# A 16-sample, two-layer transformer kernel on one core: reciprocal deviations into PSUM, and a new written-out order of calls on every engine

## The reference

```python
h = _layernorm(x) * (1 + ca) + sa
x = x + ga * _L0_attn_ref(h, ...)      # 16 heads of 16, q/k normed, causal softmax
h = _layernorm(x) * (1 + cb) + sb
x = x + gb * _L0_ffn_ref(h, ...)       # 256 -> 1024 -> 1024 -> 1024 -> 256
...                                    # layer 1, with its own modulation:
x = x + ga * _L1_attn_ref(h, ...)      # h = A_bar*h + B_bar*x over t, 512 channels, 16 states
x = x + gb * _L1_ffn_ref(h, ...)       # rows and weights rounded to a 6-bit grid in blocks of 32
```

## Time and profile before

| what | value |
|---|---|
| median of three runs | 4414.48 us (4412.8 to 4420.98) |
| the profiled execution | 4410.43 us, its span 4408.7 us |
| TensorE busy | 3700.5 us, 84% of the span |
| VectorE busy | 3558.4 us, 81% |
| GpSimd busy | 2530.8 us, 57% |
| ScalarE busy | 2435.4 us, 55% |

### The profile page before, as it was taken

The page is one execution under the profiler, slowest core; times in us unless marked ns, Lnnn a source line. Parts: engine busy times, 40 slices in busy tenths (PEclk is TensorE's granted clock), DMA queues, the critical chain, the costliest instruction groups (busy, mean ns, idle before and its releaser), DMA issues. The chain is left out here.

```text
span 4408.7 us, 51342 instructions
## 1 busy us (share of the span) xinstructions
PE 3700.5 (84%) x17261; PEld 2188.9 (50%) x17261; DVE 3558.4 (81%) x3917; ACT 2435.4 (55%) x3413; POOL 2530.8 (57%) x1895
## 2 busy tenths in 40 slices
PE   5688888989899898989888898989989898998623
PEld 3364544636464554636464463646455463646301
DVE  4514788979898887989888897989889898988795
ACT  2344555647565565646555564656556564655532
POOL 0131756648484755758474674848475574847462
PEclk8697999999999999999999999999999999999856
DMA  4630211203030110203020120303011020302000
GB/s 176 228 106 1 78 34 39 77 6 111 1 101 15 63 53 25 92 6 111 1 90 27 38 78 6 111 1 101 15 63 53 26 90 6 111 1 87 15 5 5
DMA packets 69436, 247.79 MB, mean 56 GB/s; under 512 B 9600, under 2 KB 10112, under 8 KB 68736
## 3 DMA queue, kind: packets, MB, share of 16 engines
q1 hardware_dynamic: 66816, 235.28, 16.1%
q10 hardware_dynamic: 2304, 8.39, 0.5%
HBM read 212.19 MB, written 31.46 MB: 55 GB/s over the span
## 5 line engine op out<-in xcount | busy, mean ns | idle before, releaser
L668 POOL TENSOR_TENSOR kept<-kept,hb 128x512 f32<-128x512 f32 x640 | 809.5, 1300 | 28.2 <-DVE hb L1821 28.2
L1812 DVE TENSOR_TENSOR_SCAN hb<-ps,hb 128x512 f32<-128x512 f32 x640 | 741.8, 1203 | 6.5 <-ACT ps L1332 5.6
L636 POOL TENSOR_TENSOR kept<-kept,hb 128x1024 f32<-128x1024 f32 x128 | 334.8, 2632 | 698.1 <-DVE hb L1756 639.1
L881 PE MATMUL ps<-hid_bhi,wring 128*128 128x512 f32 x1536 | 623.2, 406 | 17.3 <-issue 13.8
L881 PE MATMUL ps<-hid_blo,wring 128*128 128x512 f32 x1536 | 608.0, 396 | 0.0
L1332 ACT ACTIVATE ps<-kept,a_neg 128x512 f32<-128x512 f32 x640 | 431.7, 691 | 263.3 <-DVE hb L1812 263.3
L621 POOL TENSOR_SCALAR_AFFINE_SELECT room<-room 128x512 f32<-128x512 f32 x256 | 237.8, 945 | 570.8 <-ACT room L1498 570.8
L1882 DVE TENSOR_REDUCE room<-ps 128x4 f32<-128x2048 f32 (+3 forms) x256 | 375.6, 1488 | 234.1 <-PE ps L1060 232.8
L881 PE MATMUL ps<-hid_ahi,wring 128*128 128x512 f32 x1280 | 514.4, 402 | 18.7 <-POOL hid_alo L683 17.9
L881 PE MATMUL ps<-hid_alo,wring 128*128 128x512 f32 x1280 | 503.5, 393 | 0.0
L1498 ACT ACTIVATE room<-ps 128x2048 f32<-128x2048 f32 (+1 forms) x192 | 305.3, 1590 | 256.7 <-PE ps L1086 256.1
(11 more groups left out here) (188 smaller groups left out, 7580.5 us busy)
## 6 DMA issues: line engine op xcount, KB each, us to landing
wring<-w_hi SPq DMA_DIRECT2D x352, 512.0 KB, 3.3
kept<-in_wffn SPq DMA_DIRECT2D x22, 512.0 KB, 6.0
w_hi<-wring SPq DMA_DIRECT2D x22, 512.0 KB, 6.9
w_lo<-wrest SPq DMA_DIRECT2D x22, 512.0 KB, 3.9
xn<-in_x_fm SPq DMA_DIRECT2D x17, 512.0 KB, 3.5
out_fm<-xc ACTq DMA_DIRECT2D x16, 512.0 KB, 5.1
room<-in_wmod SPq DMA_DIRECT2D x2, 1536.0 KB, 8.2
win<-in_win SPq DMA_DIRECT2D x1, 1024.0 KB, 8.4
```

The lines of the kernel that those rows point to most:

```text
L636: pool.tensor_tensor(pair_of(acc, h), pair_of(acc, h), pair_of(hb, h), ALU.add).then_inc(tail_acc, 2)
L668: pool.tensor_tensor(acc[:, m, :], acc[:, m, :], hb[:, s % 8, :], ALU.add).then_inc(acc_done, 1)
L881: mm = pe.matmul(bank(bk), wring[:, r % 3, at + k * P:at + (k + 1) * P], src[i][:, k, :], start=(k == 0 and i == 0), stop=(k == K - 1 and ...
L1812: dve.tensor_tensor_scan(hb[:, s % 8, :], bank(2 + m % 2), hb[:, s % 8, :], 0.0, ALU.mult, ALU.add).then_inc(scanned, 1)
```

## The change

Two parts. First, `Exp` of each layer norm writes the reciprocal deviation over the variance in its PSUM bank, and the scale reads it from there. The bank is free only after the scale, so `gate_in(1)` now waits for `ln_norm` instead of `ln_log`. Second, the calls of all four pass functions are put in another order; no call is added or dropped.

```diff
-        def dve_scale(dve, k):
+        def dve_scale(dve, k, bk):
             dve.wait_ge(ln_rstd, k.number)
-            dve.tensor_tensor(ln_x[:, :, :], ln_x[:, :, :], bcast_c(ln_s[:, 1, :]), ALU.mult).then_inc(ln_norm, 1)
+            dve.tensor_tensor(ln_x[:, :, :], ln_x[:, :, :], bcast_c(bank(bk)), ALU.mult).then_inc(ln_norm, 1)
...
-            act.activation(ln_s[:, 1, :], ln_s[:, 0, :], ACT.Exp, scale=-0.5).then_inc(ln_rstd, 1)
+            act.activation(bank(bk), ln_s[:, 0, :], ACT.Exp, scale=-0.5).then_inc(ln_rstd, 1)
...
-                        pe.wait_ge((ln_cent, ln_log)[m], k_pre.number)
+                        pe.wait_ge((ln_cent, ln_norm)[m], k_pre.number)
```

The parts of the new order that the prediction speaks of, GpSimd first, then VectorE at the start of a pass and around the feed-forward net's start:

```diff
             times_b(2, 3)
             add(2, 0)
+            add(2, 1)
+            times_b(3, 3)
             split_hid(0)
-            times_b(3, 3)
-            add(2, 1)
             split_hid(1)
-            times_b(4, 3)
             split_hid(2)
             split_hid(3)
+            add(3, 0)
             split_hid(4)
             split_hid(5)
             split_hid(6)
             split_hid(7)
-            add(3, 0)
+            times_b(4, 3)
             add(3, 1)
...
             pick_mod()
             split(0)
+            pre_centre()
             tail_in(0, 0)
+            tail_scan(0, 0)
+            normalise(0)
             tail_in(0, 1)
-            tail_scan(0, 0)
+            normalise(1)
             tail_scan(0, 1)
-            normalise(0)
-            normalise(1)
-            pre_centre()
             normalise(2)
             normalise(3)
+            pre_scale()
+            find_max(0, 0)
             split(1)
             tail_out(0, 0)
             tail_out(0, 1)
-            find_max(0, 0)
+            find_max(0, 1)
...
+            invert(3)
             head_out(1, 0)
-            invert(3)
-            head_scan(1, 1)
             weigh(3)
-            head_out(1, 1)
+            quant_at(1, 0, 1, 2)
             att_add(0)
             att_add(1)
-            quant_at(1, 0, 1, 2)
+            quant_at(1, 4, 5, 6, 7, 8, 9, 10, 11)
+            ffn_centre()
+            head_scan(1, 1)
+            head_out(1, 1)
+            ffn_scale()
             times_b(2, 0)
-            ffn_centre()
-            quant_at(1, 4, 5, 6, 7, 8, 9, 10, 11)
+            scan(2, 0)
             times_b(2, 1)
...
             gate_up(3)
-            scan(3, 0)
+            scan(3, 1)
             gate_up(4)
```

More of the change, by code:

```diff
@@ L750, in gpsimd_pass @@
             add(4, 0)
+            add(4, 1)
             times_b(5, 3)
-            add(4, 1)
-            times_b(6, 3)
             split_hid(9)
             split_hid(10)
+            times_b(6, 3)
             split_hid(11)
             add(5, 0)
+            split_hid(12)
             add(5, 1)
@@ L776, in gpsimd_pass @@
             add(9, 0)
+            add(9, 1)
+            split_hid(20)
             times_b(10, 3)
-            split_hid(20)
-            add(9, 1)
             split_hid(21)
@@ L1234, in tensor_pass @@
             up(0)
+            spread(0, 3)
             up(1)
@@ L1967, in vector_pass @@
             tail_out(0, 1)
-            find_max(0, 0)
+            find_max(0, 1)
             split(2)
             tail_in(1, 0)
-            find_max(0, 1)
+            find_max(0, 2)
             split(3)
-            tail_in(1, 1)
-            find_max(0, 2)
+            shift_q(0)
             split(4)
-            pre_scale()
-            shift_q(0)
-            split(5)
             tail_scan(1, 0)
             find_max(1, 0)
-            split(6, 7)
+            split(5, 6, 7)
+            tail_in(1, 1)
+            tail_scan(1, 1)
             tail_out(1, 0)
-            tail_scan(1, 1)
             tail_out(1, 1)
@@ L1993, in vector_pass @@
             tail_out(2, 0)
+            tail_out(2, 1)
             shift_q(1)
             split(11)
-            tail_out(2, 1)
+            tail_in(3, 0)
             find_max(2, 0)
-            split(12, 13)
-            tail_in(3, 0)
+            split(12, 13, 14)
             tail_in(3, 1)
@@ L2002, in vector_pass @@
             tail_scan(3, 1)
+            tail_out(3, 0)
             find_max(2, 1)
-            split(14)
-            tail_out(3, 0)
             split_bc()
-            tail_out(3, 1)
             invert(0)
             split(15)
+            tail_out(3, 1)
             gate_out(0)
-            find_max(2, 2)
             weigh(0)
             split(16)
+            find_max(2, 2)
+            split(17, 18)
             gate_out(1)
             gate_out(2)
+            gate_out(3)
             shift_q(2)
-            split(17)
-            gate_out(3)
+            split(19)
+            out_add(0)
+            clip_dt()
             find_max(3, 0)
-            split(18, 19)
-            clip_dt()
-            out_add(0)
+            split(20, 21)
             out_add(1)
+            head_in(0, 0)
+            fin_centre()
+            head_in(0, 1)
             find_max(3, 1)
-            split(20)
-            fin_centre()
-            head_in(0, 0)
-            head_in(0, 1)
+            head_scan(0, 0)
             invert(1)
-            split(21)
-            head_scan(0, 0)
+            head_out(0, 0)
+            fin_scale()
+            weigh(1)
             find_max(3, 2)
-            fin_scale()
-            head_out(0, 0)
-            weigh(1)
             head_scan(0, 1)
             head_out(0, 1)
-            quant_at(0, 0, 1, 2)
             shift_q(3)
@@ L2082, in vector_pass @@
             times_b(5, 0)
+            scan(4, 1)
+            times_c(4, 0)
+            times_c(4, 1)
             times_b(5, 1)
[L2084 to L2086 removed]
             scan(5, 0)
+            times_c(5, 0)
+            scan(5, 1)
+            times_c(5, 1)
             times_b(6, 0)
             times_b(6, 1)
[L2090 to L2092 removed]
             scan(6, 0)
```

282 lines of the change are left out of this document (136 added, 146 removed).

## The result

The changed kernel takes 4272.6 us (median of four runs, 4268.7 to 4273.9), the old one beside it 4413.6 us (4407.2 to 4421.0). The ratio is 0.9678, 95% interval [0.9662, 0.9695]: 3.2% faster, where 0.4% was forecast and 1.7% was the edge of the range. The prediction had the direction right and the size wrong, and not by its size alone: one of its steps had the wrong sign.

A forecast was written before the change was run, and what follows sets the result against it. It took TensorE to bound the mids, and TensorE and VectorE in turn the front. Terms summed to -1.2 us a pass, times 14 -17, about -2 elsewhere: 4395 us, 0.4% faster; range 4337 to 4440 us.

The forecast's parts named there:

- Boundary: At the pass boundary, next_scale reading PSUM no longer loses time beside GpSimd, wholly on the path: -1.33 us a pass.
- Start: From the pass start to find_max(0, 0): VectorE waits for att_norm and deviations in the new order, +1.6 us a pass.
- middle: From find_max(0, 0) to the end of head_out(0, 1): half-size calls fill waits for scores, -2.2 us a pass.
- a debt of 1.2 us: At find_max(0, 0), the walked new order is 0.9 us early but VectorE owes 1.2 us more work: +0.3.
- End of the front: From head_out(0, 1) to gate_up(0): new idle times on VectorE and a late up(1) lose the lead, +2.0 us a pass.
- Up stage: From gate_up(0) to the end of mid(0): more GpSimd adds ahead of the last splits, +1.3 us a pass.
- Clock: One to two of TensorE's half-clock stretches go as its gaps in the middle shrink: -2.6 us a pass.
- the prediction's signs: Trace marks listed to show the steps, such as scales at about 1.21 us, find_max(0, 0) at T+22, mids solid for 69 us.
- VectorE idle before `att_add`: Sign in the end of the front: VectorE waits there in the new order, walked at 1.5 us.
- its own sign of being wrong: The prediction is wrong if the pass is more than 3 us shorter or the solid mids break up.
- Rival A: Slower, chance 0.28: TensorE's half-clock stretches do not shrink, +1.4 us a pass, 4433 us.
- Rival B: Much faster, chance 0.16: all four middle half-clock stretches go and waits for scores nearly close, -5.4 a pass, 4337 us.

The follow-up runs named there:

- e1: Old order of calls, with three of the four scales reading PSUM (pre_scale stays in SBUF), against the old kernel: 4384.1 us, 0.9928.
- e2: The changed kernel's new order, with the reciprocal deviations back in SBUF as before: 4317.3 us, 0.9778.
- e5: e1 with the four spread_sums copies of a pass moved from GpSimd to ScalarE: 4339.7 us, 0.9826.
- e13: The changed kernel with head_scan(1, 0) right behind invert(2) and head_scan(1, 1) right behind invert(3): 4314.4 us, 0.9762.
- e14: The changed kernel with head_scan(1, 1) and head_out(1, 1) right behind weigh(3), ahead of the quantisation and att_add: 4334.8 us, 0.9807.
- e6: e1 with five unused products in TensorE's idle time, two behind ffn_mean and three behind ffn_var: 4395.7 us, 0.9956.

## Why the prediction was wrong

Step by step, in us a pass, from the table:

- **Boundary, -1.33.** Right in mechanism, too small: of the earlier trace rows's 2.33 and 1.86 us of idle, 0.53 us and none are left (`project(0)` starts 1.6 earlier), and the scales inside the pass were in part on the path too. PSUM gives 1.7 to 2.0 in the old order (e1) and 2.8 to 3.1 in the new one (e2 to after), more than the scales themselves lose there. All 65 scales take 1.22 us; `Exp` into PSUM takes 602 ns against 631 into SBUF.
- **Start, +1.6, and middle, -2.2.** The forecast's two terms count a debt of 1.2 us that the table's columns don't. In its columns the forecast was -0.9 for the front, boundary included (`find_max(0, 0)` at 22.0 against 22.9), and -1.0 for the middle, -1.9 together. Measured: -1.6 and -3.3, together -4.9. Direction right, more than half of the size missed. 1.8 us of it comes with PSUM alone (e1). The waits for scores fell from 13.1 to 4.9 us; the wait for `out_proj`, of which half was to close, did not. The old walk is at 110.3 at the end of `head_out(0, 1)` and the old trace at 112.6, so it was already 2.3 us short there; the new walk, 108.4, is 1.0 us late.
- **End of the front, +2.0.** -4.5. This is the step that failed. I held the new walk, 151.9, against a walk of the old order, 151.8, while the trace of the old kernel had 160.7 at that place. I put the 8.9 us between them down to "mostly the half-clock stretches and GpSimd contention" and let the new order keep all of them but the 2.6 of the clock term. The new kernel keeps none: its trace is at 151.3. Of the 8.9 us, 6.6 lie in this stretch (48.1 in the trace, 41.5 in the walk), while the new one was walked at 43.5 and takes 44.0. What the old walk had left out was, at least in part, the order's own cost. Two copies took 2.6 and 2.5 us instead of 0.6, because a scan stood behind the reciprocal; the prediction does not list the lengths of its walk; if it had them at 0.6, these two alone make 3.9 of the 6.6 us. Taking them away is worth 2.6 us a pass in the old order (e5), and putting them back, with the moved scan, costs 3.5 in the new one (e13). And holding `head_scan(1, 1)` back, whose gain I saw but let new idle times eat up, is worth 1.8 to 3.4 (e14). The two overlap, so that together they give 4.5.
- **Up stage, +1.3.** The delay of `mid(0)` came (1.0 us), but the stretch to the next T is as long as before: something behind `mid(0)` gave it back. What, no run shows.
- **Clock, -2.6.** The mean granted clock rose from 0.919 to 0.925. The half-clock time of a pass fell from 22.2 to 18.3 us, and the fall is in the middle (7.9 to 2.7), where it is worth some 0.7 to 1 us (estimate above); in the end of the front it did not shrink, and the 4.5 us were won without it. So the term had the right sign and about a third of its size.

Set side by side, the forecast was -1.9 (front and middle), +2.0, +1.3 and -2.6 for the clock, together -1.2; measured are -4.9, -4.5 and 0.0 with whatever the clock gave inside, together -9.3 before rounding. Of the prediction's signs, all came but one (VectorE idle before `att_add`), and so did its own sign of being wrong, a pass more than 3 us shorter.

Rival A was right about the end of the front, where the half-clock time did not shrink; its slower time fell with the other terms of the sum.

Rival B named the waits for scores, which are a part of it; but its -5.4 is the forecast's sum with the whole 6.8 us of the clock, and that did not come. The matmuls of the mean behind a 4.42 us gap took 3.06 us in e14, against 1.88 in the changed kernel. By the Trainium skill ("TensorE: Matmul & The Clock Gate", section "HAM oscillation — how this bites in real kernels"), in a kernel that waits for its data in every turn of its loop the work behind each wait starts cold. Behind this gap the trace agrees. But in the changed kernel the end of the front has the lower clock, 0.85, and the shorter time, so the clock did not decide that stretch.

What stays open: how the 3.1 us of start and middle divide among their single moves, and how much of them is the clock; the experiments only show that start and middle come as a pair. Open, too, is why PSUM is worth 3.1 us a pass in the new order, where its scales lose 1.2.

## What to carry to other kernels

When a hand walk of the old kernel falls short of its trace, don't subtract walk from walk: find the instructions that take longer in the trace than in the walk, since they may be exactly what a new order removes. Look for slow instances of an instruction on both engines that read SBUF at the time: a group's mean of 1523 ns over instances of 0.61 and 2.6 us says that a neighbour in time costs you, and a list of who started just before names it. Then follow the chain behind the next norm or reduction, and move what it does not need behind its first link. And when idle time is filled to test the clock, look at when the next real work starts: a filler in front of it can cost what the clock gives.

## What the hardware showed unexpectedly

- A GpSimd copy (128x512, SBUF to SBUF) started just behind a VectorE scan with two SBUF inputs ends only after it: 2.5 to 2.6 us instead of 0.61. The other way round, a scan started 0.68 us behind the start of GpSimd's `head_add` (2.35 us) took 3.81 us instead of 2.28 (e14).
- The three 128x12 copies of the modulation columns (SBUF to SBUF) take 3.00 us at the new pass boundary and took 0.94 at the old one; in the mean of the steady passes 2.4 and 1.2 us, and 2.3 in e1, so this comes with PSUM and not with the order. In the changed kernel's pass they end with the second of GpSimd's two `MEMSET` of 128x2048 and 128x1024:

```profile
1534.77 1.80 POOL L611 MEMSET room<- 128x2048 f32 x1
1536.51 0.95 POOL L612 MEMSET room<- 128x1024 f32 x1
```

  In the old kernel the scale with its 2.54 us held them back, and they end with the first `MEMSET` (1586.80 against 1586.75). So at this place a part of what the PSUM operand saved went to the next instruction; `att_norm` needs only the first copy and did not notice (it starts at 1534.82).
- Raising TensorE's mean granted clock by 0.015 with unused products (e6) gained nothing: `fin_ff` took 2.2 us less and started 2.05 us later.
